# Scores with the keys stationary: a small attention without transposed probabilities

## The reference

```
q = _to_heads(plin(xm, w_q, b_q))      # the same for k and v
qt, kt, vt = (logmap0(q), logmap0(k), logmap0(v))
scores = jnp.einsum('bhqd,bhkd->bhqk', qt, kt) / math.sqrt(HD)
attn = jax.nn.softmax(scores, axis=-1)
out_h = expmap0(jnp.einsum('bhqk,bhkd->bhqd', attn, vt))
attn_out = plin(_from_heads(out_h), w_o, b_o)
```

## Time and profile before

| | us |
|---|---|
| time, median of 3 runs | 201.25 |
| lowest and highest run | 200.45, 202.8 |
| span of the profiled execution | 202.0 |
| busy in it: TensorE products, weight loads | 143.9, 117.0 |
| busy: VectorE, ScalarE, GpSimd | 127.0, 104.3, 49.7 |
| mean granted TensorE clock (1 is 2.4 GHz) | 0.823 |

### The profile page before, as it was taken

One profiled execution on the slowest core, in us unless ns is written; L12 is line 12 of the kernel. 1 busy time (PEld: TensorE's weight loads), 2 busy tenths in 40 slices (PEclk: granted clock), 3 DMA queues, 4 the chain that ended last, 5 costly groups with the idle time before them and its releaser, 6 DMA issues.

```text
span 202.0 us, 3395 instructions
## 1 busy us (share of the span) xinstructions
PE 143.9 (71%) x1252; PEld 117.0 (58%) x1252; DVE 127.0 (63%) x455; ACT 104.3 (52%) x227; POOL 49.7 (25%) x47
## 2 busy tenths in 40 slices
PE   0345957528186037598592399899899999999994
PEld 0324543327064036357281248689699798999994
DVE  0866589889839977545988999676446450221531
ACT  2366331462623577505955855998834974522400
POOL 0500004046019701000202053020001004999400
PEclk9999988856955555555879557999999999999999
DMA  6908001540499000000000000000000000000012
GB/s 185 377 23 193 15 0 52 141 70 18 118 259 338 6 0 2 3 0 0 0 0 0 2 3 0 0 0 5 0 0 0 5 0 0 0 3 0 0 29 78
DMA packets 10432, 9.71 MB, mean 48 GB/s; under 512 B 768, under 2 KB 8352, under 8 KB 10416
## 3 DMA queue, kind: packets, MB, share of 16 engines
q1 hardware_dynamic: 9952, 8.95, 15.7%
q10 hardware_dynamic: 464, 0.55, 0.9%
HBM read 8.42 MB, written 1.08 MB: 47 GB/s over the span
## 4 chain that ended last, share of the span: by engine, by line
PE 49%; DVE 35%; ACT 8%; issue 3%; DMA 2%; POOL 2%; ACTq 0%; DVEq 0%
PE bank L1244 18%; PE bank L1228 4%; PE bank L1230 4%; PE bank L1229 4%; PE bank L1070 4%; PE bank L1164 3%; DVE qkv L463 3%; PE bank L1100 3%; PE bank L1158 2%; DMA col<-cols 2%; PE bank L1194 2%; PE bank L1082 2%; DVE qkv L468 2%; DVE prob L538 2%; POOL st L994 2%
## 5 line engine op out<-in xcount | busy, mean ns | idle before, releaser
L632 DVE SCALAR_TENSOR_TENSOR xn<-bank,wtok,xn 128x128 f32<-128x128 f32 x32 | 9.0, 344 | 22.0 <-PE bank L1244 21.9
L878 ACT ACTIVATE probT<-bank,col 128x512 f32<-128x512 f32 x24 | 15.6, 688 | 9.1 <-PE bank L1230 9.0
L1133 PE MATMUL bank<-cst,prob 128*128 128x128 f32 x32 | 7.4, 424 | 14.6 <-ACT prob L792 14.6
L1228 PE MATMUL bank<-x3hi,whi 128*128 128x512 f32 x40 | 16.9, 422 | 0.7 <-ACT probT L878 0.7
L1164 PE MATMUL bank<-yT,wf 128*128 128x512 f32 x16 | 12.9, 913 | 4.7 <-DVE yT L360 4.2
L1230 PE MATMUL bank<-x3lo,whi 128*128 128x512 f32 x40 | 15.7, 391 | 0.0
L1229 PE MATMUL bank<-x3hi,wlo 128*128 128x512 f32 x40 | 15.6, 391 | 0.0
L1133 PEld LDWEIGHTS bank<-cst,prob 128*128 128x128 f32 x32 | 6.6, 227 | 15.3 <-ACT prob L792 15.3
L878 ACT ACTIVATE prob<-bank,col 128x512 f32<-128x512 f32 x16 | 10.8, 689 | 8.6 <-PE bank L1230 8.6
L1244 PE MATMUL bank<-vexp,prob 128*128 128x128 f32 x128 | 15.0, 276 | 0.0
L1244 PEld LDWEIGHTS bank<-vexp,prob 128*128 128x128 f32 x128 | 14.8, 192 | 0.3
(11 more groups left out here) (196 smaller groups left out, 355.3 us busy)
## 6 DMA issues: line engine op xcount, KB each, us to landing
vrep<-v_dram SPq DMA_DIRECT2D x8, 256.0 KB, 4.2
vrep<-w_up SPq DMA_DIRECT2D x5, 256.0 KB, 5.1
gain<-gain_dram SPq DMA_DIRECT2D x4, 256.0 KB, 5.2
vexp<-w_down SPq DMA_DIRECT2D x4, 256.0 KB, 7.1
row<-rows SPq DMA_DIRECT2D x1, 774.0 KB, 6.3
xin<-x SPq DMA_DIRECT2D x2, 256.0 KB, 3.6
wf<-w_f SPq DMA_DIRECT2D x2, 256.0 KB, 6.5
v_dram<-vs SPq DMA_DIRECT2D x2, 256.0 KB, 2.5
```

Of the source, the lines that this page charges most:

```text
L878: act(hT[e % 2][:, g, c, :], bk(g, (e * FC + c) % 3)[:, :], ACT.Gelu_apprx_tanh, bias=col[:, K_EB1 + e * FC + c:K_EB1 + e * FC + c + 1]).t ...
L1133: last = tr(bk(g, n)[:, t * P:(t + 1) * P], prob[:, g, n, t * P:(t + 1) * P], ident)
L1228: mm(z, hi[:, c * P:(c + 1) * P], xhi, start=True, stop=False)
```

## The change

q becomes the moving side and kexp the stationary one: kexp of one set and sequence (32 rows by 128 columns) is loaded as weights, and the 32 queries of the sequence move. So heads and keys are on the output partitions, and the exponentials can be used as they are as the stationary side of weigh_v. transpose_probs and copy_probs go. The keys are expanded on ScalarE, one copy per head over all 16 sequences, with the mask as its scale. The values are clamped on VectorE, repeated over the partitions by a product with a constant 0/1 matrix (replicate_v, weights 32 rows by 128 columns, 128 columns moving), and masked by VectorE on the way out of PSUM (expand_v, four steps of 512 columns). GpSimd's two steps and the way through memory go, and SP loads the up weights as soon as the space is free. The layout of vexp changes to [b, t, n], and the order of the banks and of the calls changes with all this: on ScalarE exps(0) and copy_o(0) move ahead of or around the squares and head norms of group 1, on VectorE head_clamps(1) moves behind heads_out(0), and on TensorE transpose_qk(1) moves behind project_out(0).

The diff, without the declarations of tiles and semaphores:

```diff
@@ -42,7 +42,7 @@
 TAIL = S - 2 * SEG
-C_ID, C_HM, C_VM, C_WM, C_TRI, C_TINY, C_END = 0, 128, 132, 136, 140, 156, 157
+C_ID, C_REP, C_HM, C_VM, C_WM, C_TRI, C_TINY, C_END = 0, 128, 256, 260, 264, 268, 284, 285
 S_SEL, S_END = 0, 512
@@ -187,7 +185,10 @@
         def bk(g, i):
             return bank[4 * g + i]
-        BANKS = [0, 2, 3, 1]
+        BANKS = [0, 3, 2, 1]
+        VBANKS = [2, 3, 0, 2]
+        VB_DONE = {0: 3, 1: 4, 2: 4, 3: 2}
+        OB = BANKS[:2]
         UPB = [3, 0, 1, 2]
         LAST = [3, 0]
@@ -234,22 +235,14 @@
                              gain_dram.rearrange("(t b) d -> b t d", b=BT)[b:b + 1].broadcast_to([S, TILES, 2 * D])) \
                     .then_inc(s["gain_in"], 16)
-            for g in range(NG):
-                sp.wait_ge(s["v_ready"][g], 1)
-                sp.dma_start(v_dram[g], vs[:, T(g), :]).then_inc(s["v_out"][g], 16)
-                sp.wait_ge(s["v_out"][g], 16)
-                for h in range(HG):
-                    sp.dma_start(vrep[h * S:(h + 1) * S, g, :, :].rearrange("s (t b) d -> s t b d", b=BT),
-                                 v_dram[g].rearrange("(b s) t d -> s t b d", b=BT)).then_inc(vrep_in[g], 16)
-            sp.wait_ge(s["vexp_ready"][0], 1)
+            sp.wait_ge(s["vals"][0], nth(VALS, "head"))
             for e in range(E):
                 load_up(e)
+            sp.wait_ge(s["vals"][1], nth(VALS, "head"))
+            load_up(E)
             sp.wait_ge(s["o_mm"][0], 1)
             for e in range(1, E + 1):
                 load_down(e)
-            sp.wait_ge(s["vexp_ready"][1], 1)
-            load_up(E)
             for g in range(NG):
                 for i in range(2):
                     sp.wait_ge(s["moe_acc"][g], E + 2 + i)
@@ -404,20 +397,24 @@
                                    qkv[:, T(g), 0:2 * D].rearrange("p t (h d) -> p t h d", d=HD),
                                    c4.unsqueeze(3).broadcast_to([P, TG, 2 * H, HD]), ALU.mult).then_inc(s["qk_ready"][g], 1)
-            def expand_k(g):
-                v.wait_ge(s["trans_mm"][g], nth(TRANS, "kT"))
-                hm = cst[:, C_HM:C_HM + HG].unsqueeze(1).broadcast_to([P, BT, HG]).unsqueeze(3).broadcast_to([P, BT, HG, S])
-                for i in range(TG):
-                    kk = bk(g, 1)[:, i * P:(i + 1) * P].rearrange("p (r s) -> p r s", s=S).unsqueeze(2) \
-                        .broadcast_to([P, BT, HG, S])
-                    nc_v.tensor_tensor(kexp[:, g, i * BT:(i + 1) * BT], kk, hm, ALU.mult).then_inc(s["kexp_ready"][g], 1)
-            def copy_probs(g):
-                for k in (0, 2):
-                    i = BANKS[k]
-                    v.wait_ge(s["pT_mm"][g], k + 1)
-                    nc_v.tensor_copy(probT[:, g, i, :], bk(g, i)[:, :]).then_inc(s["pT_even"][g], 1)
+            def clamp_v(g):
+                v.wait_ge(s["c_ready"][g], 1)
+                c = heads[:, g, 3, 0:n_hd].rearrange("p (t h) -> p t h", t=TG)[:, :, 2 * H:3 * H]
+                nc_v.tensor_tensor(vs[:, T(g), :].rearrange("p t (h d) -> p t h d", d=HD),
+                                   qkv[:, T(g), 2 * D:3 * D].rearrange("p t (h d) -> p t h d", d=HD),
+                                   c.unsqueeze(3).broadcast_to([P, TG, H, HD]), ALU.mult).then_inc(s["v_ready"][g], 1)
+            def expand_v(g, bs):
+                n = TG * NHG
+                vm = cst[:, C_VM:C_VM + HG].unsqueeze(1).broadcast_to([P, n, HG]).unsqueeze(3).broadcast_to([P, n, HG, HD])
+                for b in bs:
+                    v.wait_ge(s["vrep_mm"][g], b + 1)
+                    nc_v.tensor_tensor(
+                        vexp[:, g, b].rearrange("p t n w -> p (t n) w")[:, :, 0:HG * HD].rearrange("p n (h d) -> p n h d", d=HD),
+                        bk(g, VBANKS[b])[:, :].rearrange("p (n h d) -> p n h d", h=HG, d=HD), vm,
+                        ALU.mult).then_inc(s["vexp_ready"][g], 1)
             def head_squares(g):
@@ -670,23 +667,24 @@
             modulate(1, 0)
             head_sums(0)
             head_clamps(0)
+            clamp_v(0)
             silu_out()
+            expand_v(0, range(BT))
             clamp_y(1, 0)
-            expand_k(0)
             project(1)
             head_sums(1)
-            head_clamps(1)
-            copy_probs(0)
-            expand_k(1)
             head_squares(0)
             heads_out(0)
+            head_clamps(1)
+            clamp_v(1)
             token_clamp(0)
             branch_out(0, 0, 3, "ap_mm", R_BO, xin)
+            expand_v(1, range(0, 2))
             branch_norm(0, 0)
             mobius(0, 0, xin, x1)
             mean_square(0, 1)
+            expand_v(1, range(2, BT))
             log_small(0, 1)
-            copy_probs(1)
             log_factor(0, 1)
             normalise(0, 1, x1)
             modulate(0, 1)
@@ -788,23 +786,25 @@
             def exps(g):
                 for k, i in enumerate(BANKS):
-                    a.wait_ge(s["sc_mm"][g], 1 if k < 3 else 2)
+                    a.wait_ge(s["sc_mm"][g], k + 1)
                     act(prob[:, g, i, :], bk(g, i)[:, :], ACT.Exp, scale=HD ** -0.5).then_inc(s["p_ready"][g], 1)
             def silu_exp():
                 act(silu[:], col[:, K_COND:K_COND + B], ACT.Exp, scale=-1.0).then_inc(s["silu_e"], 1)
-            def copy_probs(g):
-                for k in (1, 3):
-                    i = BANKS[k]
-                    a.wait_ge(s["pT_mm"][g], k + 1)
-                    act(probT[:, g, i, :], bk(g, i)[:, :], ACT.Copy).then_inc(s["pT_odd"][g], 1)
+            def expand_k(g, hs):
+                a.wait_ge(s["trans_mm"][g], nth(TRANS, "kT"))
+                kk = bk(g, 1)[:, :].rearrange("p (r s) -> p r s", s=S)
+                for h in hs:
+                    act(kexp[:, g, :, h, :], kk, ACT.Copy,
+                        scale=cst[:, C_HM + h:C_HM + h + 1]).then_inc(s["kexp_ready"][g], 1)
             def copy_o(g):
                 a.wait_ge(s["o_mm"][g], 1)
                 for i in range(2):
                     t = g * TG + 2 * i
-                    act(o[:, t:t + 2].rearrange("p t n w -> p (t n w)"), bk(g, i)[:, 0:2 * NHG * VW],
+                    act(o[:, t:t + 2].rearrange("p t n w -> p (t n w)"), bk(g, OB[i])[:, 0:2 * NHG * VW],
                         ACT.Copy).then_inc(s["o_ready"][g], 1)
                 a.wait_ge(s["o_ready"][g], 2)
                 act(osq[:, T(g), :].rearrange("p t (n w) -> p (t n) w", w=HG * HD),
@@ -898,21 +898,22 @@
             head_norms(0)
             norm_y(1, 0)
             copy_qT(0)
+            expand_k(0, range(HG))
+            exps(0)
             square_qkv(1)
+            copy_o(0)
             head_norms(1)
-            exps(0)
-            copy_probs(0)
-            copy_o(0)
             out_norms(0)
-            copy_qT(1)
             copy_ainT(0)
             token_norms(0)
+            copy_qT(1)
+            expand_k(1, range(0, 2))
             branch_squares(0, 0)
             tanh_norm(0, 0)
+            expand_k(1, range(2, HG))
             branch_scaled(0, 0)
             exps(1)
             logs(0, 1)
-            copy_probs(1)
             rstd(0, 1)
             normalise(0, 1, x1)
             copy_o(1)
@@ -994,22 +995,6 @@
                 nc_p.tensor_tensor(st[:, j, 2, T(g)], st[:, j, 1, T(g)], half[:].broadcast_to([P, TG]), ALU.pow) \
                     .then_inc(s["rms_ready"][g], 1)
-            def clamp_v(g):
-                p.wait_ge(s["c_ready"][g], 1)
-                c = heads[:, g, 3, 0:TG * 3 * H].rearrange("p (t h) -> p t h", t=TG)[:, :, 2 * H:3 * H]
-                nc_p.tensor_tensor(vs[:, T(g), :].rearrange("p t (h d) -> p t h d", d=HD),
-                                   qkv[:, T(g), 2 * D:3 * D].rearrange("p t (h d) -> p t h d", d=HD),
-                                   c.unsqueeze(3).broadcast_to([P, TG, H, HD]), ALU.mult).then_inc(s["v_ready"][g], 1)
-            def expand_v(g):
-                vd = vexp[:, g].rearrange("p r n w -> p (r n) w")
-                p.wait_ge(vrep_in[g], 16 * HG)
-                nc_p.tensor_tensor(vd[:, :, 0:HG * HD].rearrange("p n (h d) -> p n h d", d=HD),
-                                   vrep[:, g].rearrange("p r (n h d) -> p (r n) h d", h=HG, d=HD),
-                                   vm.unsqueeze(1).broadcast_to([P, n, HG]).unsqueeze(3).broadcast_to([P, n, HG, HD]),
-                                   ALU.mult).then_inc(s["vexp_ready"][g], 1)
             def split_up(e):
                 p.wait_ge(w_in[e], 32)
@@ -1031,10 +1016,6 @@
             start()
             root_mean_square(1, 0)
             root_mean_square(0, 0)
-            clamp_v(0)
-            expand_v(0)
-            clamp_v(1)
-            expand_v(1)
             split_up(0)
             split_up(1)
             split_up(2)
@@ -1112,39 +1093,42 @@
                 for half in range(2):
                     transpose_group(bk(g, half), qk[:, :, half * D:(half + 1) * D], g)
+            def replicate_v(g, bs):
+                pe.wait_ge(s["v_ready"][g], 1)
```

(57 more changed lines are left out.)

20 lines of the change are left out of this document (9 added, 11 removed).

## The result

The changed kernel takes 238.4 us (median of 6 runs, 236.82 to 241.13) against 202.69 us (median of 6, 200.45 to 202.84) for the kernel before on the same chip: a ratio of 1.1786, 95% interval 1.1722 to 1.185. The profiled execution of the changed kernel has a span of 235.0 us and took 236.82 us, its fastest. A span is not a time: in the runs recorded with experiments 1 to 12, the kernel before takes 1.97 to 2.16 us more than its span. By that its profiled execution, span 202.0 us, took some 204.0 us (an estimate), more than any of its six runs.

A forecast was written before the change was run, and what follows sets the result against it. It took a relay of engines waiting on each other as the bound until TensorE's expert matmuls. Marker 69.2 + 256 p, less 3.2, gives 119.8, 38.4 us later; span 240.4, less 0.75, is 239.6 us, range 216 to 249.

The forecast's parts named there:

- The 0.75 us taken off: Profiled execution's span lies 0.75 us over the runs' median of 201.25, so that was subtracted from forecast times.
- the marker: Start of TensorE's xn transpose for group 0's second half, 81.44 us before; its delay was to delay the end equally.
- The formula: Marker = 69.2 + 256 p us, p being the price of one score record; 119.8 after 3.2 off for full clock.
- the tail: From the end of group 1's scores to the marker: last exponential 0.6 and 4.8 from the table load, 5.4 us.
- price p: Cost of one score record on TensorE, set by its weight load: 0.210 us at half clock, 0.111 at full.
- Rival C: Row tiling makes 32-row score loads cheap, 29 ns a record: marker 4.8 us earlier, 196 us; chance 0.05.
- Rival B: Clock stays up through group 0's scores, 0.111 us a record: marker 16.9 us later, 218 us; chance 0.15.
- Rival D: Score loads wait for their row group's products, 0.265 us a record: marker 52.4 us later, 254 us; chance 0.08.
- The holds: GpSimd two-input operations hold VectorE; two, 2.8 us in head_clamps(1) and 2.9 us at 60.31, were to go.
- split 0: GpSimd's first up-weight split, to come at about 34 to 36 us in group 0's masking, costing 0.7 us.
- Splits 1 and 2: GpSimd's next two up-weight splits, to fall into group 0's output branch and cost 1.9 us.
- Nearly one chain: Work between group 0's scores and group 1's scores, across ScalarE and VectorE, summed as nearly one chain: 25.7 us.

The follow-up runs named there:

- e4: Changed kernel with 64 instead of 32 query columns moved in each score record: 238.69 us.
- e3: Changed kernel with score loads of 64 instead of 128 columns, leaving out two of four heads of each set: 215.06 us.
- e2: Changed kernel with score records alternating between two row groups, then between the other two: 216.41 us.
- e1: Changed kernel with the four row groups taking turns record by record in the scores: 207.72 us, ratio 1.0224 to the kernel before.
- e6: Changed kernel with the squares of group 1 ahead of group 0's exponentials on ScalarE: 239.13 us.
- e7: Changed kernel with all that group 1 needs for its scores moved under group 0's scores or into gaps: 229.05 us.
- e5: Kernel before with only the values' path changed (VectorE clamp and masks, TensorE replication, up weights loaded early): 201.8 us, ratio 0.9978.
- e9: Changed kernel with four row groups in turn, group 1's preparation moved earlier, and GpSimd's up-weight splits held until group 1's ain: 198.33 us, ratio 0.978 to the kernel before.
- e8: Changed kernel with four row groups in turn in the scores and group 1's preparation moved earlier: 200.61 us, ratio 0.9897 to the kernel before.
- e10: Kernel e9 with group 0's second half ahead of group 1's exponentials on ScalarE and weighing on TensorE: 201.5 us, ratio 0.9972 to the kernel before.

## Why the prediction was right

The forecast was 239.6 us and the time 238.4. The mechanism is the one named: the scores cost their weight loads, one behind the other. The agreement is better than its parts, and in part luck. By differences the forecast is +38.4 us, the medians +35.7, the profiled spans +33.0; the kernel before ran 1.4 us slower in the later runs than in those that the forecast was tied to. The 0.75 us taken off compared a span with a time. Held against times, the execution read was some 2.8 us over the median of 201.25 (204.0, the estimate above), and the new span of 240.4 would be a time of 242.2; less 2.8 that is 239.4, so two slips of 2 us cancel. The error in the span, 5.4 us, is 3.1 at the marker and 2.3 behind it.

*The formula held.* With the two measured score times in place of 256 p: 69.2 + 22.5 + 25.0 = 116.7, against a marker at 116.74. It holds within 2 us for variants that keep the order (e4 is experiment 4, and so on): e4 118.3 by the formula and 116.63 measured, e3 93.8 and 93.01, e2 92.6 and 93.88, and less well e1, 83.3 and 85.87, where the four exponentials and the fourth mask are what it lacks. Its stretches: start of scores(0) 38.02 (38.1 forecast), from there to scores(1) 25.96 (25.7), the tail 5.23 (5.4).

*The price p was mis-sized, 5 to 8% too high.* In place of 0.210 us a record at half clock came 0.195 over the 128 of group 1 (25.0 us for 26.9); group 0 took 22.5 us for 23.7. Inside a bank the step was 0.213, near the 0.207 read off the small products; the rest is the overlap at the three changes of row group, 0.8 us each, which the prediction set to nothing. "All 32 records of one n stay in one row group, so I give them no overlap beyond what that row has" was right of the 32 (e1, e2); that the group is changed three times was overlooked. The first 3 us at full clock were as forecast, and saved 2.5 us (22.5 against 25.0) where 3.2 were put. That was this execution's: in e6 and e7 the clock was at half from the start of scores(0) (0.50 from 38 to 61 us), and they took 24.98 and 25.00 us.

*Rows of weights don't make a load cheaper, columns do.* The step from a 16-row load to a 32-row one was sound (0.213 us inside a bank), and e3 shows the columns. What the row of 16 could not show, and what decides how bad this change is, is the row group. Rival C asked for under 48 ns a record to break even. Four groups in turn reach 55 ns even at half clock, and with that alone the kernel is 2.2% slower (e1, interval 1.0 to 3.5%). I wrote of C that the 16-row load spoke against it; that speaks only for loads issued one after another in one group.

*Rival B* (clock up) didn't happen: 0.50 in both scores but for the first 2.7 us. It also stayed at 0.50 in e1, where loads and products were three to four times as dense. *Rival D* fell with e4.

*Behind the marker* "nothing changes" held as far as the change goes. The 2.3 us there are the granted clock's: the kernel before was at half right after the marker, this execution at full from some 6 us behind it, and e4, with the same work behind the scores, at half for as long as the kernel before (120.3 us to the end). A forecast in spans has this spread of some 2 us in it, whatever the sum.

*The holds.* Both large ones went, as said. The splits' own were priced about right for 1 and 2 and misplaced, and split 0 was not on the path in this execution. Split 0 was put in expand_v(0) at 0.7 us; it came at 31.37 and lengthened L396 and L404 by 0.4 and 1.1. VectorE was through with L404 at 34.04, before TensorE had ended its projection and transposes. Those ran late by the clock (5.47 us for 4.40), and so the replication started at 34.79 for 33.85; it took 3.1 us for 3.6, and with the 0.7 put for split 0 the errors cancel in the start of the scores (38.02, forecast 38.1). That is luck. Splits 1 and 2 were put in branch_out at 1.9 us; they came some 5 us sooner, beside group 1's clamps, where L391 and L396 lost 0.3 and 1.0 us, and branch_out ran in 2.9. The path is the same there, so the sum didn't notice.

*"Nearly one chain"* between the scores was right as a sum and not as a reason. E6 shows that its first part had two ways of equal length. E7 shows that 10 us of the whole were on the path by order only.

*The gains.* The values' part was credited with the end of two holds (5.7 us) against masks and a replication. Alone, in the order of the kernel before, it changes nothing (e5). So rival C's 196 us counted a gain that e5 doesn't show. With scores at 7.05 us a group it took e7's order and e9's late splits to reach 198.33.

*Left open:* what the gaps of 1.3 to 1.4 us inside weigh_v in e8 and e10, and inside scores(1) of the kernel before, wait for; whether the PSUM bank has a part in the queueing; and why the clock stays at half under dense loads. Keys on ScalarE were not tried alone; their four copies took 2.41 us in group 0, beside TensorE's replication.

## What to carry to other kernels

Where a small product swaps its operands, price it by the columns of its weights, and then look at the order: loads of 32 rows by 128 columns that alternate between row groups run side by side, those that stay in one queue up, by a factor of 3.5 here (25.0 us against 7.05). A hold removed from an engine counts only if what replaces it isn't on the same engine ahead of the same wait; and a span's sum of steps says nothing on how much of it is there by the order of the lists alone. Weigh against the interleaving that the first result is then ready only with the last. And before a difference between two profiled executions is put down to an edit, look at the granted clock of both and at a third: here 2 to 3 us of such differences were the clock's alone.

## What was not expected of the hardware

- Weight loads of 32 rows by 128 columns, at a granted clock of 0.50: 0.213 us apart in one row group, 0.102 in two, 0.055 in four. The Trainium skill (TensorE: Matmul & The Clock Gate, LDWEIGHTS) gives columns / 1.2 in ns, 107 ns for 128. That agrees with no row here at half clock, but with those at full clock; at half clock it is about twice that. Its statement that a 32-row load takes as long as a 128-row one is borne out.
- Loads in one row group run under that group's products: doubling the moved columns from 32 to 64 cost 0.15 us in 128 records (e4).
- TensorE was 100% busy by its records for 22 and 25 us, with the granted clock at 0.50 but for the first 2.7 us; in e1, with 24 loads a microsecond, it was at 0.50 as well.
